# Who starts the first six query transfers of batch 1's cross attention: ScalarE or the sync engine

## The chip, the cores and the metric

The kernel runs on one core of a Trainium2 chip. The metric is the device time of one execution, in microseconds (us), and the time of a kernel is the median of several executions.

## The reference, cut to what matters

The whole computation is a chain of eight blocks on an input of two batches of 512 tokens with 128 features. Blocks 4 and 6 (counted from 0) are transformer stacks of six layers each, and the change lives in their layers, twelve in all. One layer is, for each batch:

```python
h = h + so_w @ attention(rope(q(n1(h))), rope(k(n1(h))), v(n1(h)))          # self: 16 heads of 8, 512 keys
h = h + co_w @ attention(rope(cq(n2(h))), rope(ck(context)), cv(context))   # cross: 154 keys
h = h + f2_w @ gelu(f1_w @ n3(h) + f1_b) + f2_b                             # feed-forward, 512 wide
```

n1, n2 and n3 are layer norms whose gain and shift depend on a condition vector. Block 0, a slot attention, is touched by the change in its semaphores alone.

## The kernel before, in words

Features lie on the 128 partitions and a batch's 512 tokens along the free axis. The kernel is written by hand as five instruction streams: TensorE (PE), VectorE (DVE), ScalarE (ACT), GpSimd (POOL) and the sync engine (SP), which only starts transfers. Semaphores join the streams. Each engine runs its own stream in order, so an instruction that waits holds up all that stands behind it on that engine.

A layer is 371 items of work (for instance a norm, a projection, a group of scores). The table PLACES (lines 85 to 137) gives each item a place in one common order, and each engine's stream is that order with the other engines' steps left out. Items of neighbouring layers may overlap: a place under 0 is done in the layer before, one from 371 on in the layer after.

**The stacking.** Attention scores are wanted almost in float32, but are computed in bf16. So a rotated query or key (L824, DVE) is split in three bf16 parts: the high part by an ACT copy (L715, item "hi"), the middle and the low part by three POOL operations (L881, L883, L886). The parts are then laid under each other on the partitions of the operand, six slots for each head, by transfers from on-chip memory to on-chip memory. For queries the high part goes to three slots, the middle one to two and the low one to one; each slot takes two transfers of 64 KB. That is twelve transfers for one batch's queries of one attention: six of part 0, four of part 1, two of part 2. They are started by `restack` (L424 to L434, the transfer itself is L433) from the items ("st", batch, unit, part), where unit 0 is the self queries, 1 the self keys, 2 the cross queries and 3 the cross keys.

Which engine starts them is set by the tuple ACT_STACKS (L436): the items in it are started by ACT (`stack`, L717 to L721), which waits for the high part first, the others by SP (L926 to L930), which waits for the part that the item needs. Before the change the tuple holds ("st", 0, 1, 0), batch 0's self keys, high part, and ("st", 1, 2, 0), batch 1's cross queries, high part.

**The order around the change.** The items are, by their places:

- 295 load sout (SP, eight transfers of weights)
- 296 proj(1,2), PE L574 and DVE L820 to L824: batch 1's cross queries
- 297 hi(1,2): ACT L715, then POOL
- 298 out(0,1): PE L536 and DVE L794, which finishes batch 0's h
- 299, 300, 301 the stack items of batch 1's cross queries, parts 0, 1 and 2
- 302 center(0,2): PE L552, ACT L694 and L695; the start of batch 0's third norm
- 303 var(0,2): PE L560, ACT L702 and L705; 304 apply(0,2): DVE L803 and L806, which makes xn
- 305 score(1,1,0,0): PE L460, the first scores of batch 1's cross attention; at this item PE waits for all twelve transfers (L442)
- 306, 308 f1(0,0) and f1(0,1): PE L616, ACT L757, with scores between them
- 316 f2(0): PE L631, DVE L849

ACT's stream holds the high part's copy, then the six transfers, then the squares of center(0,2). PE's stream holds center, var, the first scores, then f1.

A PE matmul of float32 operands shows as two instructions in the profile, so that f1(0,0), two matmuls, is "x4", and f2, four matmuls, "x8".

Of the kernel before, what the change touches and what calls it, by code (L numbers as in the profile page):

```python
# [253 lines left out]
def build(nc, dram):  # L254

    with ExitStack() as ctx:
# [176 lines left out]
                        eng.dma_start((kst if u == 1 else qst)[b][rows, :, :], unit_parts(b, u)[r::2, part, :])\  # L433
                           .then_inc(stacked(b, u), 16)  # L434

        ACT_STACKS = (("st", 0, 1, 0), ("st", 1, 2, 0))  # L436

        def stack_pe_items(pe, z):
            def score(it):
# [521 lines left out]
        def x_is(v):  # L961

            def wait(eng, b):
# [24 lines left out]
        sigma0 = carve(8)  # L988
        ITERS = 3
        s0 = {k: sem("slot_" + k) for k in  # L990
              ("loaded", "zeroed", "gained", "fold_mm", "folded", "kv_mm", "kv_out", "sigma", "slots", "q_mm", "q_scaled",
               "q_out", "logit_mm", "max", "max_scaled", "exp", "sum_inv", "attn", "col_mm", "upd_mm", "col_log", "col_inv",
               "upd_out", "lin_mm", "lin_out", "resid")}
        PER_ITER_RESID = 4
# [12 lines left out]
        def fold_pe(pe):  # L1007
            pe.wait_ge(s0["loaded"], 48)
            pe.transpose(bank(4)[:, 0:P], w0[:, WV], ident).then_inc(s0["fold_mm"], 1)
            pe.transpose(bank(5)[:, 0:P], bv_rows, ident).then_inc(s0["fold_mm"], 1)  # L1010
            pe.matmul(bank(6)[:, P:P + 1], w0[:, WQ], vec(V_QB), start=True, stop=True)
            pe.wait_ge(s0["gained"], 1)
            pe.matmul(bank(6)[:, 0:P], center, wq_gain, start=True, stop=True).then_inc(s0["fold_mm"], 1)
            pe.wait_ge(s0["folded"], 1)
            pe.matmul(bank(7)[:, 0:P], wv_turned, w0[:, WU], start=True, stop=True)
            pe.wait_ge(s0["folded"], 2)
            pe.matmul(bank(7)[:, P:2 * P], bv_turned, w0[:, WU], start=True, stop=True).then_inc(s0["fold_mm"], 1)
# [12 lines left out]
        def b0_pe(pe, c):  # L1030
            ln_pe(pe, c["ln"], x, x_is(c["x"]))
            fold_pe(pe)
            pe.wait_ge(loaded, LOADED)
            ln_pe(pe, c["ln"] + 1, ctxT[:, :], lambda eng, b: eng.wait_ge(ln_done, 2 * c["done"] + 2), width=CTX)
            pe.wait_ge(ln_done, 2 * c["done"] + 4)
            pe.wait_ge(s0["folded"], 6)
            pe.matmul(bank(4)[:, 0:B * CTX], w0[:, WK], ctxn, start=True, stop=True).then_inc(s0["kv_mm"], 1)
            for b in range(B):
                for k in range(KC):
                    n = key_rows(k)  # L1040
                    mm = pe.matmul(bank(5)[0:n, (2 * b + k) * P:(2 * b + k + 1) * P],
                                   ctxn[:, b * CTX + k * P:b * CTX + k * P + n], wvu, start=True, stop=True)
            mm.then_inc(s0["kv_mm"], 1)
            for t in range(ITERS):
                n = c["ln"] + 2 + 3 * t
                d = 2 * (c["done"] + 2 + t)
                for b in range(B):
                    slots_are(t)(pe, b)
                    pe.matmul(bank(b), center, cols(h, b), start=True, stop=True).then_inc(ln_centered, 1)
                for b in range(B):  # L1050
                    pe.wait_ge(ln_squared, 2 * n + b + 1)
                    pe.matmul(bank(2 + b), mean_w, cols(sq, b), start=True, stop=True).then_inc(ln_variance, 1)
                    pe.matmul(bank(6 + b), wq_fold, cols(h, b), start=True, stop=True).then_inc(s0["q_mm"], 1)
                pe.wait_ge(s0["kv_out"], 2)
                for b in range(B):
                    pe.wait_ge(s0["q_out"], 2 * t + b + 1)
                    for k in range(2 * b, 2 * b + 2):
                        n_rows = key_rows(k)
                        pe.matmul(bank(4 + k)[0:n_rows, :], key0[:, b * CTX + (k % 2) * P:b * CTX + (k % 2) * P + n_rows],
                                  cols(q0, b), start=True, stop=True).then_inc(s0["logit_mm"], 1)  # L1060
                pe.wait_ge(s0["zeroed"], 2)
                for b in range(B):
                    pe.wait_ge(s0["attn"], 4 * t + 2 * b + 2)
                    for k in range(KC):
                        mm = pe.matmul(bank(2 + b), mean_w, attn0[:, 2 * b + k], start=(k == 0), stop=(k == 1))
                    mm.then_inc(s0["col_mm"], 1)
                    for k in range(KC):
                        mm = pe.matmul(bank(b), val0[:, b, k], attn0[:, 2 * b + k], start=(k == 0), stop=(k == 1))
                    mm.then_inc(s0["upd_mm"], 1)
                ln_pe(pe, n + 1, h, lambda eng, b: eng.wait_ge(s0["resid"], PER_ITER_RESID * t + b + 1))  # L1070
                for b in range(B):
                    pe.wait_ge(ln_done, d + b + 1)
                    pe.matmul(bank(4 + b), w0[:, W1], cols(xn, b), start=True, stop=True).then_inc(s0["lin_mm"], 1)
                for b in range(B):
                    pe.wait_ge(s0["lin_out"], 2 * t + b + 1)
                    pe.matmul(bank(6 + b), w0[:, W2], cols(hid0, b), start=True, stop=True).then_inc(s0["lin_mm"], 1)
                ln_pe(pe, n + 2, h, lambda eng, b: eng.wait_ge(s0["resid"], PER_ITER_RESID * t + 2 + b + 1))

        def b0_act(act, c):
            ln_act(act, c["ln"])  # L1080
            act.wait_ge(s0["loaded"], 48)
            act.activation(sigma0[:, 0:1], vec(V_SIG), ACT.Exp).then_inc(s0["sigma"], 1)
            fold_act(act)
            ln_act(act, c["ln"] + 1, width=CTX)
            act.wait_ge(s0["kv_mm"], 1)
            act.activation(key0, bank(4)[:, 0:B * CTX], ACT.Identity, bias=vec(V_BK)).then_inc(s0["kv_out"], 1)
            for t in range(ITERS):
                n = c["ln"] + 2 + 3 * t
                ln_act(act, n)
                for k in range(4):  # L1090
                    r = key_rows(k)
                    act.wait_ge(s0["max_scaled"], 4 * t + k + 1)
                    act.wait_ge(s0["zeroed"], 2)
                    act.activation(attn0[0:r, k], bank(4 + k)[0:r, :], ACT.Exp, bias=smx0[0:r, k:k + 1],
                                   scale=float(D) ** 0.5, accum_out=sum0[0:r, k:k + 1]).then_inc(s0["exp"], 1)
                for b in range(B):
                    act.wait_ge(s0["col_mm"], 2 * t + b + 1)
                    act.activation(cols(lg, b), bank(2 + b), ACT.Ln).then_inc(s0["col_log"], 1)
                    act.wait_ge(s0["col_log"], 2 * t + b + 1)
                    act.activation(cols(rstd, b), cols(lg, b), ACT.Exp, scale=-1.0).then_inc(s0["col_inv"], 1)  # L1100
                ln_act(act, n + 1)
                for b in range(B):
                    act.wait_ge(s0["lin_mm"], 4 * t + b + 1)
                    act.activation(cols(hid0, b), bank(4 + b), ACT.Gelu, bias=vec(V_B1)).then_inc(s0["lin_out"], 1)
                both_log_and_exp(act)
                ln_act(act, n + 2)

        def b0_dve(ve, c):
            ve.memset(val0[:, :, :, :], 0.0).then_inc(s0["zeroed"], 1)
            ve.memset(attn0[:, :, :], 0.0).then_inc(s0["zeroed"], 1)  # L1110
            ve.wait_ge(s0["loaded"], 48)
            ve.tensor_scalar(wq_gain, w0[:, WQ], vec(V_QG), None, ALU.mult).then_inc(s0["gained"], 1)
            ln_dve(ve, c["ln"], xn)
            ve.wait_ge(s0["sigma"], 1)
            for b in range(B):
# [1 line left out]
                ve.tensor_scalar(cols(h, b), cols(xn, b), sigma0[:, 0:1], vec(V_MU), ALU.mult, ALU.add)\  # L1117
                  .then_inc(s0["slots"], 1)
            ve.wait_ge(loaded, LOADED)
            ve.tensor_scalar(b2_cond[:, 0:B], condT[:, :], vec(V_B2), None, ALU.add).then_inc(s0["gained"], 1)  # L1120
            ln_dve(ve, c["ln"] + 1, ctxn, gain=lambda b: vec(V_KG), shift=lambda b: vec(V_KB), width=CTX,
                   scaled=c["scaled"])
            ve.wait_ge(s0["kv_mm"], 2)
            ve.wait_ge(s0["zeroed"], 2)
            ve.wait_ge(s0["folded"], 6)
            ve.wait_ge(s0["gained"], 2)
            for k in range(4):
                r = key_rows(k)
                op = ve.tensor_tensor(val0[0:r, k // 2, k % 2], bank(5)[0:r, k * P:(k + 1) * P], bvu_rows[0:r, :], ALU.add)
# [18 lines left out]
            for t in range(ITERS):  # L1148
                n = c["ln"] + 2 + 3 * t
                sc = c["scaled"] + 1 + 2 * t  # L1150
                for b in range(B):
                    ve.wait_ge(ln_rstd, 2 * n + b + 1)
                    ve.wait_ge(s0["q_mm"], 2 * t + b + 1)
                    ve.tensor_tensor(cols(qraw0, b), bank(6 + b), cols(rstd, b), ALU.mult).then_inc(s0["q_scaled"], 1)
                    ve.wait_ge(s0["q_scaled"], 2 * t + b + 1)
                    ve.tensor_scalar(cols(q0, b), cols(qraw0, b), bq_fold[:, 0:1], None, ALU.add).then_inc(s0["q_out"], 1)
                largest(t, 0)
                largest(t, 1)
# [1498 lines left out]
```

## Time and profile before

| | |
|---|---|
| median of 3 runs | 3646.8 us (3642.5 to 3654.24) |
| the profiled execution's own time | 3644.69 us |
| its span, first to last instruction | 3642.9 us |
| mean granted TensorE clock | 0.916 of full speed |
| PE busy | 2960.6 us, 81% |
| DVE busy | 1979.4 us, 54% |
| ACT busy | 1896.2 us, 52% |
| POOL busy | 805.7 us, 22% |
| transfers L433 started by SP | 720 |
| transfers L433 started by ACT | 144 |

Busy time counts arithmetic alone: starting a transfer is not in it, though the engine can do nothing else meanwhile. In rows of the profile, "SPq" and "ACTq" are such starts. A row of the timeline merges like instructions in a row: start, length, engine, line, operation, output and inputs, count, and in brackets the idle time just before and what ended it. "issue" there means that the engine waited for nothing that the profile shows as a releaser.

### The profile page before, as it was taken

To read this page: it belongs to the slowest core of one execution; us is meant where nothing else is said; L and a number is where in the kernel's file an instruction comes from. 1 tells how busy PE (TensorE), PEld (TensorE's weight loads), DVE (VectorE), ACT (ScalarE), POOL (GpSimd) and SP (SyncE) were. 2 spreads that over 40 slices of the span, in tenths; PEclk is the share of its full clock that TensorE was granted. 3 is DMA by queue.
4 is the path that set the end of the run, shared out by engine and by line. 5 is a ranking of instruction groups with operands and counts; after the bars stand their busy time and mean duration, and the time that the engine had idled before them with its cause. 6 is when DMAs were issued, how large, how long until landed. Compare 5 with 4: busy or idle time off the path is not lost.

```text
span 3642.9 us, 50334 instructions
## 1 busy us (share of the span) xinstructions
PE 2960.6 (81%) x15559; PEld 1013.4 (28%) x15559; DVE 1979.4 (54%) x3535; ACT 1896.2 (52%) x2677; POOL 805.7 (22%) x1327
## 2 busy tenths in 40 slices
PE   7899999868788787887878746878788787887866
PEld 2463333222222222222222211222222222222225
DVE  4324444248375573756648366558375664846524
ACT  5432333327556474665747534647466574665632
POOL 0003444512212122122222102212212222222211
PEclk9999999979989898998989877989899998999977
DMA  1100000001110111101011001001110111101030
GB/s 41 53 18 6 1 1 1 10 20 39 33 35 24 36 36 32 36 27 48 20 36 41 22 8 43 25 29 41 33 35 27 38 30 31 42 23 48 24 115 7
DMA packets 125570, 110.74 MB, mean 30 GB/s; under 512 B 49982, under 2 KB 116076, under 8 KB 125292
## 3 DMA queue, kind: packets, MB, share of 16 engines
q1 hardware_dynamic: 114924, 97.80, 9.1%
q10 hardware_dynamic: 10368, 9.44, 0.8%
q8 instruction: 148, 2.42, 0.3%
q14 instruction: 130, 1.06, 0.1%
HBM read 41.96 MB, written 0.52 MB: 12 GB/s over the span
## 4 chain that ended last, share of the span: by engine, by line
PE 65%; DVE 15%; issue 7%; ACT 7%; POOL 3%; ACTq 2%; SPq 1%; DMA 0%; DVEq 0%; POOLq 0%
PE ps L508 11%; DVE arena L783 7%; PE ps L453 5%; PE ps L482 4%; PE ps L631 3%; PE ps L616 3%; PE ps L574 3%; PE ps L536 3%; PE ps L1452 3%; ACT arena L656 3%; PE ps L560 3%; PE ps L1468 3%; PE ps L525 2%; PE ps L552 2%; PE ps L516 2%
## 5 line engine op out<-in xcount | busy, mean ns | idle before, releaser
L656 ACT ACTIVATE arena<-ps 128x1024 f32<-128x1024 f32 x960 | 936.4, 1024 | 344.0 <-PE ps L482 340.3
L783 DVE TENSOR_REDUCE arena<-ps 128x1 f32<-128x512 f32 x1536 | 966.1, 683 | 207.1 <-PE ps L453 186.5
L508 PE MATMUL ps<-arena 128*32 128x512 f32 x3840 | 513.2, 609 | 20.5 <-ACT arena L656 18.0
L453 PE MATMUL ps<-arena 49*128 49x512 bf16 x1536 | 317.7, 410 | 239.5 <-DVE arena L783 198.4
L482 PE MATMUL ps<-arena 52*128 52x512 bf16 x1920 | 346.1, 387 | 28.7 <-ACT arena L656 25.2
L785 DVE TENSOR_REDUCE arena<-ps 128x3 f32<-128x462 f32 (+1 forms) x576 | 303.1, 579 | 108.7 <-PE ps L460 104.9
L865 POOL TENSOR_TENSOR arena<-arena,zeros 128x16 bf16<-128x16 f32 x192 | 42.3, 220 | 1078.7 <-DVE arena L783 636.7
L453 PEld LDWEIGHTS ps<-arena 49*128 49x128 bf16 x1536 | 75.2, 94 | 590.1 <-DVE arena L783 493.4
L875 POOL TENSOR_TENSOR arena<-arena 128x512 f32<-128x512 f32 x96 | 121.9, 1270 | 453.2 <-ACT arena L688 453.2
L881 POOL TENSOR_TENSOR arena<-arena 128x512 bf16<-128x512 f32 (+1 forms) x84 | 92.4, 1100 | 546.8 <-ACT arena L715 546.8
L803 DVE SCALAR_TENSOR_TENSOR tmp<-tmp,arena,rstd 128x512 f32<-128x512 f32 x72 | 54.1, 751 | 270.2 <-ACT rstd L705 267.9
L794 DVE TENSOR_TENSOR h<-ps,h 128x512 f32<-128x512 f32 x48 | 33.2, 692 | 299.1 <-PE ps L536 299.1
L1519 ACT ACTIVATE arena<-ps 128x1024 f32<-128x1024 f32 x96 | 98.0, 1021 | 177.7 <-PE ps L1456 141.7
L482 PEld LDWEIGHTS ps<-arena 52*128 52x128 bf16 x1920 | 86.8, 94 | 311.5 <-ACT arena L656 195.8
L536 PE MATMUL ps<-arena,w 128*128 128x512 f32 x192 | 128.8, 808 | 50.7 <-issue 23.8
L1680 POOL TENSOR_TENSOR arena<-arena 128x1024 f32<-128x1024 f32 x64 | 150.0, 2344 | 64.7 <-ACT arena L1519 64.2
L694 ACT ACTIVATE sq<-ps 128x512 f32<-128x512 f32 x76 | 45.2, 594 | 214.0 <-PE ps L552 160.6
L574 PE MATMUL ps<-xn,w 128*128 128x512 f32 x288 | 144.4, 627 | 8.0 <-DVE xn L806 7.4
L460 PE MATMUL ps<-arena 49*128 49x154 bf16 x1536 | 104.8, 237 | 56.1 <-DVE arena L785 38.3
L616 PE MATMUL ps<-xn,w 128*128 128x512 f32 x192 | 122.3, 772 | 20.7 <-DVE xn L806 20.7
L1587 DVE TENSOR_REDUCE arena<-ps 128x1 f32<-128x512 f32 x128 | 82.5, 686 | 101.9 <-PE ps L1420 101.9
L525 PE MATMUL ps<-arena,selector 128*128 128x512 f32 x192 | 106.8, 638 | 37.7 <-ACT arena L675 32.0
(379 smaller groups left out, 4185.7 us busy)
## 6 DMA issues: line engine op xcount, KB each, us to landing
arena<-arena SPq DMA_DIRECT2D x720, 64.0 KB
arena<-we_dram SPq DMA_DIRECT2D x24, 578.5 KB, 7.7
arena<-arena ACTq DMA_DIRECT2D x144, 64.0 KB
w<-weights_dram SPq DMA_DIRECT2D x26, 320.0 KB, 3.1
w<-weights_dram SPq DMA_DIRECT2D x13, 512.0 KB, 3.7
arena<-arena SPq DMA_DIRECT2D x384, 6.0 KB
arena<-arena SPq DMA_DIRECT2D x288, 19.2 KB
w<-weights_dram SPq DMA_DIRECT2D x39, 128.0 KB, 2.1
```

Of the source, the lines that this page charges most:

```text
L453: pe.matmul(s_bank(slot + r), qst[b][rows, idx, P * qt:P * (qt + 1)], kst[b][rows, idx, :], start=True, stop=True).then_inc(s_full, 1 + (z ...
L482: mm = pe.matmul(e_bank(slot)[:, S * r:S * (r + 1)], (kst, kstc)[a][b][rows, 2 * g + p, P * kt:P * (kt + 1)], qst[b][rows, 2 * g + p, :], ...
L508: mm = pe.matmul(bank(7)[32 * j:32 * j + 32, :], v, prob[:, slot, j, :], start=(g % 2 == 0 and kt == 0), stop=(a == 0 and g % 2 == 1 and k ...
L525: pe.matmul(e_bank(slot)[:, 0:S], selector2[:, :], osb[:, e, :], start=True, stop=True)\
L536: mm = pe.matmul(s_bank(slot), w[:, base + P * e:base + P * (e + 1)], att[:, b, e, :], start=(e == 0), stop=(e == 1))
L574: pe.matmul(s_bank(slot + i)[:, 0:B * CTX if u == 3 else S], w[:, base + P * i:base + P * (i + 1)], src, start=True, stop=True).then_inc(s ...
L616: mm = pe.matmul(e_bank(slot)[:, S * i:S * (i + 1)], w[:, W_F1 + P * t:W_F1 + P * (t + 1)], cols(xn, b), start=True, stop=True)
L656: act.activation(prob[:, chunk_no(b, a, g, kt) % NPROB, 2 * p:2 * p + 2, :], e_bank(slot).rearrange("p (j n) -> p j n", j=2), ACT.Exp, sca ...
L783: op = ve.tensor_reduce(nmax[:, g % 2, r, n:n + 1], s_bank(slot + r), AX.X, ALU.max, negate=True)
L785: op = ve.tensor_reduce(nmax[:, g % 2, r, 3 * n:3 * n + pack(n)], s_bank(slot + r)[:, 0:pack(n) * CTX].rearrange("p (i n) -> p i n", n=CTX ...
L875: gp.tensor_tensor(att[:, b, e, :], osb[:, e, :], rinv[:, e, :], ALU.mult).then_inc(att_ready, 1)
L1680: gp.tensor_tensor(sum2[0:n, :, :], sum2[0:n, :, :], prob2[0:n, j], ALU.add).then_inc(s2["summed"], 1)
```

## The change

The item ("st", 1, 2, 0) leaves ACT_STACKS: SP starts the six transfers of batch 1's cross queries' high part, at the same place 299 of its own order, and ACT no longer does. In block 0 semaphores are joined: "zeroed" and "gained" become "made", "q_scaled" and "q_out" become one, with the counts waited for adapted.

```diff
-        ACT_STACKS = (("st", 0, 1, 0), ("st", 1, 2, 0))
+        ACT_STACKS = (("st", 0, 1, 0),)
...
-              ("loaded", "zeroed", "gained", "fold_mm", "folded", "kv_mm", "kv_out", "sigma", "slots", "q_mm", "q_scaled",
+              ("loaded", "made", "fold_mm", "folded", "kv_mm", "kv_out", "sigma", "slots", "q_mm",
...
-            pe.wait_ge(s0["gained"], 1)
+            pe.wait_ge(s0["made"], 3)
...
-                    pe.wait_ge(s0["q_out"], 2 * t + b + 1)
+                    pe.wait_ge(s0["q_out"], 2 * (2 * t + b + 1))
...
-                pe.wait_ge(s0["zeroed"], 2)
+                pe.wait_ge(s0["made"], 2)
...
-            ve.memset(val0[:, :, :, :], 0.0).then_inc(s0["zeroed"], 1)
-            ve.memset(attn0[:, :, :], 0.0).then_inc(s0["zeroed"], 1)
+            ve.memset(val0[:, :, :, :], 0.0).then_inc(s0["made"], 1)
+            ve.memset(attn0[:, :, :], 0.0).then_inc(s0["made"], 1)
             ve.wait_ge(s0["loaded"], 48)
-            ve.tensor_scalar(wq_gain, w0[:, WQ], vec(V_QG), None, ALU.mult).then_inc(s0["gained"], 1)
+            ve.tensor_scalar(wq_gain, w0[:, WQ], vec(V_QG), None, ALU.mult).then_inc(s0["made"], 1)
...
-            ve.tensor_scalar(b2_cond[:, 0:B], condT[:, :], vec(V_B2), None, ALU.add).then_inc(s0["gained"], 1)
+            ve.tensor_scalar(b2_cond[:, 0:B], condT[:, :], vec(V_B2), None, ALU.add).then_inc(s0["made"], 1)
...
-            ve.wait_ge(s0["gained"], 2)
+            ve.wait_ge(s0["made"], 4)
...
-                    ve.tensor_tensor(cols(qraw0, b), bank(6 + b), cols(rstd, b), ALU.mult).then_inc(s0["q_scaled"], 1)
-                    ve.wait_ge(s0["q_scaled"], 2 * t + b + 1)
+                    ve.tensor_tensor(cols(qraw0, b), bank(6 + b), cols(rstd, b), ALU.mult).then_inc(s0["q_out"], 1)
+                    ve.wait_ge(s0["q_out"], 2 * (2 * t + b) + 1)
```

## Rows read from the trace of the kernel before

**Rows 1.** The page: the span, and the chain of waits by engine.

```profile
span 3642.9 us, 50334 instructions
...
PE 65%; DVE 15%; issue 7%; ACT 7%; POOL 3%; ACTq 2%; SPq 1%; DMA 0%; DVEq 0%; POOLq 0%
```

**Rows 2.** Waits, whole span: who waited for whom, us in total, times, longest.

```profile
ACT sq L694 <- issue: 52.8, 12, 4.4
...
PE ps L616 <- DVE xn L806: 17.9, 13, 2.8
PE ps L460 <- DMA arena<-arena: 12.3, 12, 1.5
```

**Rows 3.** Timeline of ACT in the second layer, around its transfers.

```profile
1164.46 0.63 ACT L715 ACTIVATE arena<-arena 128x512 bf16<-128x512 f32 x1 [2.05 <-DVE arena L824]
1165.12 4.28 ACTq L433 DMA_DIRECT2D arena<-arena  x6
1169.52 0.60 ACT L694 ACTIVATE sq<-ps 128x512 f32<-128x512 f32 x1 [4.42 <-issue]
```

**Rows 4.** Timeline of PE in the same layer.

```profile
1166.66 1.12 PE L552 MATMUL ps<-h,consts 128*128 128x512 f32 x2 [0.86 <-DVE h L794]
1170.24 1.12 PE L560 MATMUL ps<-sq,consts 128*128 128x512 f32 x2 [2.46 <-ACT sq L694]
1172.72 0.57 PE L460 MATMUL ps<-arena 49*128 49x154 bf16 x6 [1.36 <-DMA arena<-arena]
1174.19 3.78 PE L616 MATMUL ps<-xn,w 128*128 128x512 f32 x4 [0.89 <-DVE xn L806]
1177.90 0.56 PE L460 MATMUL ps<-arena 49*128 49x154 bf16 x6
1178.39 1.98 PE L616 MATMUL ps<-xn,w 128*128 128x512 f32 x4
```

**Rows 5.** Timelines of SP and POOL in the same layer.

```profile
1166.35 4.15 SPq L433 DMA_DIRECT2D arena<-arena  x6
...
1167.57 1.15 POOL L886 TENSOR_TENSOR arena<-arena 128x512 bf16<-128x512 f32 x1
```

**Rows 6.** Line L433, whole span: ns of one start, least/median/most; first and last.

```profile
L433 SPq DMA_DIRECT2D arena<-arena x720: 607/608/1462, 779.3 to 3456.3; - x180
L433 ACTq DMA_DIRECT2D arena<-arena x144: 622/708/1219, 782.9 to 3455.2; - x144
```

**Rows 7.** Timeline of SP, where it starts ten and twelve transfers on its own.

```profile
1050.16 6.53 SPq L433 DMA_DIRECT2D arena<-arena  x10
...
1071.96 7.88 SPq L430 DMA_DIRECT2D arena<-arena  x12
```

**Rows 8.** Timelines of SP and PE at the first stack's start.

```profile
779.31 12.11 SPq L433 DMA_DIRECT2D arena<-arena  x18
...
793.18 0.61 PE L453 MATMUL ps<-arena 49*128 49x512 bf16 x2 [13.31 <-DMA arena<-arena]
```

**Rows 9.** ACT and PE timelines in the first layer and the last (twelfth).

```profile
947.58 4.31 ACTq L433 DMA_DIRECT2D arena<-arena  x6
...
955.19 0.57 PE L460 MATMUL ps<-arena 49*128 49x154 bf16 x6 [1.02 <-DMA arena<-arena]
...
3451.65 4.27 ACTq L433 DMA_DIRECT2D arena<-arena  x6
...
3459.29 0.56 PE L460 MATMUL ps<-arena 49*128 49x154 bf16 x6 [1.54 <-DMA arena<-arena]
```

**Rows 10.** DMA by stretch: us, five engines' busy, PEclk, DMA share, GB/s.

```profile
1166.40:1170.50 4.10, 1.38 (x3) 0.56 (x4) 0.13 (x1) 0.98 (x2) 2.18 (x2) 1.00 0.45 137
1051.20:1056.70 5.50, 5.04 (x31) 1.30 (x23) 5.07 (x9) 3.15 (x4) 3.26 (x7) 1.00 0.33 96
```

**Rows 11.** f2 by stretch, second and third layer; columns as in rows 10.

```profile
1184.01:1187.70 3.69, 3.69 (x9) 1.50 (x9) 0.64 (x2) 0.00 (x0) 0.83 (x4) 1.00 0.35 92
...
1403.01:1408.40 5.39, 5.39 (x9) 2.09 (x9) 0.64 (x2) 0.00 (x0) 0.83 (x4) 0.68 0.24 63
```

More of the change, by code:

```diff
@@ L1092, in b0_act @@
                     act.wait_ge(s0["max_scaled"], 4 * t + k + 1)
-                    act.wait_ge(s0["zeroed"], 2)
+                    act.wait_ge(s0["made"], 2)
                     act.activation(attn0[0:r, k], bank(4 + k)[0:r, :], ACT.Exp, bias=smx0[0:r, k:k + 1],
@@ L1123, in b0_dve @@
             ve.wait_ge(s0["kv_mm"], 2)
-            ve.wait_ge(s0["zeroed"], 2)
+            ve.wait_ge(s0["made"], 2)
             ve.wait_ge(s0["folded"], 6)
-            ve.wait_ge(s0["gained"], 2)
+            ve.wait_ge(s0["made"], 4)
             for k in range(4):
```

## The prediction, made before the changed kernel was seen

> **What bounds the kernel now.** I began with the page's chain of waits [rows 1]. PE carries 65% of the chain, but 2% of it is ACTq, ACT starting transfers: such starts lie on the path that sets the end. The list of waits says where [rows 2]. ACT's squares at L694 stood behind "issue" 12 times, 52.8 us in total, 4.4 us each, once in each layer of the two stacks. In the same places PE waits for transfers before its first cross scores (L460, 12 times, 12.3 us) and for xn before f1 (L616, 17.9 us in 13 waits; the longest, 2.8 us, lies between the stacks, the twelve of the layers sum to 15.1 us).
>
> The timelines of the second layer show how these hang together. I count from the start of ACT's six transfers, 1165.12, as zero.
>
> - ACT: the high part's copy is done at 0, its six starts last to 4.28, and the squares begin at 4.40 [rows 3]. PE had delivered their input at 2.66 (1166.66 + 1.12 = 1167.78) [rows 4]. So center(0,2) loses 4.40 - 2.70 = 1.70 us to the starts.
> - SP: it starts its own six, parts 1 and 2, at 1.23, when POOL has the middle part, and is done at 5.38 [rows 5]. The last one opens PE's wait at 7.60, 2.22 us later, and the first scores run [rows 4, 5].
> - f1 starts at 9.07, held by xn, which stems from the squares; PE idles 0.89 us in front of it [rows 4].
>
> So two legs run side by side and meet at f1: ACT's leg (starts, squares, var, xn) ends at 9.07, the transfers' leg (SP's starts, landing, scores) would allow f1 at 7.60 + 0.49 = 8.09. The 0.49 is what f1(0,1) stands behind the scores ahead of it at the same low clock (1178.39 - 1177.90) [rows 4]. The leg of ACT is the later one now, by about 1 us.
>
> **Part 1, what is taken from ACT.** Six starts of 0.708 us [rows 6], 4.28 us a layer. The squares begin 1.70 us earlier, at 2.70, as L552's end sets it, and xn is ready near 9.07 - 1.70 = 7.37. The rest of the freed time covers nothing: ACT's next work needs f1. Worth at most 1.7 us a layer, and only if nothing else holds f1.
>
> **Part 2, what is given to SP.** SP waits for the high part at place 299 (its loads for sout are long done) and can begin at 0.03. It has then all twelve to start. A start lasts 0.608 us on SP at the median [rows 6], but they don't stand back to back: ten of this very kind took 6.53 us, twelve others 7.88 us, 0.66 us each [rows 7]. The middle part is ready at 1.2 and the low part at 3.60 (1167.57 + 1.15 - 1165.12) [rows 5], well before SP gets to them after six and ten starts, so no data wait remains. SP is done at 0.03 + 7.88 = 7.91, against 5.38 before: 2.53 us later. Nothing else of SP's stands in the way or is needed soon; its next step is a row for scores that are not yet computed.
>
> **Part 3, from the last start to PE.** The trace has two values. In the layers, with ACT and SP both starting, it is 2.22 us. At the start of the first stack, where SP alone starts the last seven or so of 18, PE goes at 793.18, 1.76 us after SP's end at 791.42 [rows 8]. The DMA engines bear this out: their share is 0.45 and 137 GB/s while two engines start, 0.33 and 96 GB/s with SP alone [rows 10], so less stands in line. After the change SP starts alone, so I take 1.76 and keep 2.22 as the bound. The first scores then start at 7.91 + 1.76 = 9.67, against 7.60 before: +2.07. Over the layers the 7.6 holds: 955.19 - 947.58 = 7.61 in the first, 3459.29 - 3451.65 = 7.64 in the last [rows 9], 7.43 to 7.68 in the ten between.
>
> **Part 4, what reaches f1.** xn, at 7.4, no longer matters; f1 follows the scores. In the second layer it starts at 9.67 + 0.49 = 10.16 against 9.07: +1.09. Over all twelve layers: the scores are 12 x 2.08 = 25.0 us later, and of that the waits for xn absorb what they sum to, 15.1 us [rows 2], and 12 x 0.07 us more (modelled ends overlap: the scores show as 0.57 but f1 can follow at 0.49 to 0.52). That leaves 25.0 - 15.1 - 0.8 = +9.1 us, 0.76 us a layer.
>
> **Part 5, what follows.** PE is in order, and behind f1 come the scores of batch 1's cross attention, f2, the next layer's norm; all of it waits for f1 directly or behind it in PE's stream. I see no later wait for something that doesn't shift, so nothing gives it back.
>
> **Part 6, the clock.** f1's first two matmuls run at 1.2 GHz already (3.78 us, against 1.98 for the second two [rows 4]), since PE was mostly idle ahead of them. After the change the idle stretches are joined: var moves to about 3.5, then PE idles from 4.6 to 9.7, and then works without a gap. So f1 is mostly at the low level before and after. f2 is the sensitive one: at 2.4 GHz it takes 3.69 us, in other layers 5.39 us with a granted clock of 0.68 [rows 11]. Five of the twelve layers are of the first kind, seven of the second. Which it is depends on when PE's work falls, so a shift of 0.8 us can flip layers both ways. I take zero; the bounds are 5 x 1.7 = +8.5 us and 7 x 1.7 = -11.9 us.
>
> **Part 7, the semaphores of block 0.** The counts open the same waits at the same instructions: wq_gain is DVE's third "made", and the two memsets precede it on DVE anyway. Nothing is added, 0 us.
>
> **The page's rule.** SP alone keeps the DMA engines a third busy [rows 10], so here the starts are the scarce thing, at 0.66 us each against six by ACT beside them. The Trainium skill, page "DMA: Bandwidth & Descriptors", section "Issuing engines are not separate DMA queues", says that all starts end on the same 16 engines, and that starting from several saves only the time of starting, "which is usually small relative to the DMA itself". The trace agrees with the first half and not with "small". By the rule at its word the landing wouldn't move, which is rival A.
>
> **The sum.** Own time 3644.7 + 9.1 = 3653.8. The median of the runs shown is 2.1 us above that execution, so 3646.8 + 9.1 = 3655.9. About 0.3%, 10.9 us (3635.9 to 3657.7), is what a measurement of this kernel can tell from no change; the forecast lies just inside, on the slow side.
>
> **Lower and upper bounds of the terms.** Starts back to back would be 12 x 0.608 = 7.30 instead of 7.88: -7.0 us in twelve layers, sum +2.1. A landing of 2.22 instead of 1.76: +5.5 us, sum +14.6.
>
> **Rivals.**
>
> A. Transfer-bound, faster. If the 16 engines and not the starts set the last landing, the scores start as before, f1 moves up to right behind them and the twelve waits for xn vanish: -15.1 - 0.8 = -15.9, 3630.9. For it: two starting engines lengthen the landing from 1.76 to 2.22. Against it: a share of 0.45 is no full queue, and SP cannot hand over its twelfth transfer before 7.3. Chance 0.05.
>
> B. The clock, slower. Its place is f2(0), L631. If the later and unbroken idle ahead of the scores makes the clock rise later relative to f1, all twelve f2 fall in the 5.39 us kind: +8.5 on top: 3646.8 + 9.1 + 8.5 = 3664.4. It decides from the point where more than one of the five fast layers flips and none flips back. For it: seven of twelve are already so. Against: nothing in the rows makes the flip one-sided. Chance 0.25.
>
> C. The clock the other way, or denser starts: seven slow f2 become fast, 3646.8 + 9.1 - 11.9 = 3644.0; or starts back to back, 3648.9. Chance 0.15.
>
> D. The forecast, 3650 to 3661: chance 0.55, of which about 0.33 lie under 3657.7.
>
> That the change does nothing can't be: the item moves in all twelve layers.
>
> **The numbers.** Faster: A, 0.05. Within 0.3%: C and the lower part of D, 0.15 + 0.33, and a little of B, 0.50 in all. Slower: the rest of D and B, 0.45. The range leaves out A and the ends of B and C: 3643 to 3666. Predicted 3655.9.
>
> **What would show it.** In the changed trace: no "issue" in front of L694, squares about 2.7 us after the copy's end; one SP row of twelve starts, 7.9 us, from the copy's end; PE's first cross scores at 9.7 after it with a wait for DMA of about 5 us; f1 right behind without a wait for xn; L631 still of both kinds. It is wrong if the scores start under 8.5 (A), if SP's twelve take 7.3, or if the period of a layer grows by anything but 0.8 us, which f2's lengths would then explain.

## The result, and the profile after

The changed kernel takes 3656.9 us (median of 12 runs, 3646.5 to 3664.1), the kernel before 3646.4 beside it (12 runs). The ratio is 1.0028, with a 95% interval from 1.0017 to 1.0038: slower by 10 us (6 to 14). Measured again beside the kernel before, the changed kernel gave 1.0012 (1.0002 to 1.0022), slower by 4 us (1 to 8). The forecast was 3655.9, on the slow side of no change.

The profiled execution took 3662.74 us, near the slow end of its runs, so I compare layer with layer and not span with span. The page, as far as it answers to [rows 1]:

```profile
span 3660.9 us, 50334 instructions
...
PE 2963.8 (81%) x15559; PEld 1015.1 (28%) x15559; DVE 1981.7 (54%) x3535; ACT 1899.6 (52%) x2677; POOL 806.0 (22%) x1327
...
PE 65%; DVE 15%; issue 7%; ACT 6%; SPq 3%; POOL 3%; DMA 1%; ACTq 0%; DVEq 0%; POOLq 0%
```

ACTq has left the chain (2% before) and SPq has grown from 1% to 3%, DMA from 0 to 1%: the starts are on the path still, under another engine's name. The waits over the whole span, and line L433 (ns of one start), against [rows 2, 6]:

```profile
ACT sq L694 <- PE ps L552: 197.8, 38, 18.5
...
PE ps L460 <- DMA arena<-arena: 61.1, 13, 5.4
...
PE ps L616 <- DVE xn L806: 5.6, 2, 2.8
...
L433 SPq DMA_DIRECT2D arena<-arena x792: 607/608/1781, 782.0 to 3475.1; - x198
L433 ACTq DMA_DIRECT2D arena<-arena x72: 622/699/1219, 784.5 to 3295.0; - x72
```

The 52.8 us of "issue" ahead of L694 are gone, its waits are for PE alone. PE's wait for transfers at L460 has grown from 12.3 to 61.1 us, to 5 us a layer. The twelve waits for xn ahead of f1 have vanished. (The row for them in [rows 2] is of the stretch of the two stacks alone, 780 to 3510 us; over the whole span the kernel before has 20.7 us in 14 waits, and the two that are left here lie outside these places.) So the later leg at f1 has changed hands. The second layer shows it in its timelines, ACT first, then PE, SP and a stretch of the DMA engines (columns as in rows 10), against [rows 3, 4, 5, 10]:

```profile
1169.55 0.63 ACT L715 ACTIVATE arena<-arena 128x512 bf16<-128x512 f32 x1 [2.06 <-DVE arena L824]
1172.90 0.60 ACT L694 ACTIVATE sq<-ps 128x512 f32<-128x512 f32 x1 [2.73 <-PE ps L552]
...
1171.75 1.12 PE L552 MATMUL ps<-h,consts 128*128 128x512 f32 x2 [0.86 <-DVE h L794]
...
1179.83 0.57 PE L460 MATMUL ps<-arena 49*128 49x154 bf16 x6 [5.08 <-DMA arena<-arena]
1180.32 3.37 PE L616 MATMUL ps<-xn,w 128*128 128x512 f32 x4
...
1183.93 1.98 PE L616 MATMUL ps<-xn,w 128*128 128x512 f32 x4
...
1189.55 5.39 PE L631 MATMUL ps<-arena,w 128*128 128x512 f32 x8 [0.31 <-DVE arena L785]
...
1170.20 7.88 SPq L433 DMA_DIRECT2D arena<-arena  x12
...
1171.50:1177.50 6.00, 2.24 (x4) 0.59 (x4) 1.35 (x3) 3.69 (x5) 2.17 (x2) 0.90 0.35 100
```

Zero here and below is 0.03 us behind the copy's end, where the first start stands or stood (1170.21 in this layer, 1165.12 in the kernel before): SP's twelve starts run to 7.87, PE sees the last transfer at 9.62, f1 starts at 10.11 with nothing between. The squares start at 2.69. The DMA engines are a third busy, at 100 GB/s.

### The profile page after: what moved, and what is told of

Read it like the earlier page. It is cut to its first block, busy times and chain, and to the rows that moved or that the text cites. A ratio compares the mean times of both kernels' runs of the same rounds, so it can differ in the third digit from the quotient of the medians.

```text
span 3660.9 us, 50334 instructions
## 1 busy us (share of the span) xinstructions
PE 2963.8 (81%) x15559; PEld 1015.1 (28%) x15559; DVE 1981.7 (54%) x3535; ACT 1899.6 (52%) x2677; POOL 806.0 (22%) x1327
## 4 chain that ended last, share of the span: by engine, by line
PE 65%; DVE 15%; issue 7%; ACT 6%; SPq 3%; POOL 3%; DMA 1%; ACTq 0%; DVEq 0%; POOLq 0%
PE ps L508 10%; DVE arena L783 7%; PE ps L453 5%; PE ps L482 4%; PE ps L616 3%; PE ps L631 3%; SPq L433 3%; PE ps L574 3%; PE ps L536 3%; PE ps L1452 3%; ACT arena L656 3%; PE ps L1468 3%; PE ps L525 2%; PE ps L560 2%; PE ps L552 2%
## 5 line engine op out<-in xcount | busy, mean ns | idle before, releaser
L460 PE MATMUL ps<-arena 49*128 49x154 bf16 x1536 | 105.0, 238 | 104.6 <-DMA arena<-arena 61.1
L574 PE MATMUL ps<-xn,w 128*128 128x512 f32 x288 | 143.4, 622 | 8.0 <-DVE xn L806 7.4
L694 ACT ACTIVATE sq<-ps 128x512 f32<-128x512 f32 x76 | 45.3, 596 | 198.3 <-PE ps L552 197.8
L820 DVE TENSOR_TENSOR arena<-ps,rope 128x512 f32<-128x512 f32 x144 | 99.5, 692 | 66.0 <-PE ps L574 63.0
```

What stands on the lines that cost most here:

```text
L574: pe.matmul(s_bank(slot + i)[:, 0:B * CTX if u == 3 else S], w[:, base + P * i:base + P * (i + 1)], src, start=True, stop=True).then_inc(s ...
```

## The experiments

All times in this table are means over the twelve layers, in us from the zero just named, read from the timelines of one profiled execution each. The ratio is to the kernel before, run on the same chip, with its 95% interval. "12 x f1" is what the shift of f1 against the 9.41 of before would give, if all behind it shifted as much. An execution that was profiled can lie some us off its kernel's median: 5.9 us above it for the changed kernel, 5.4 and 8.5 above with three and five starts by ACT.

| kernel | starts by ACT / SP | squares | scores | f1 | f2 ends | slow f2 | 12 x f1 | ratio |
|---|---|---|---|---|---|---|---|---|
| before | 6 / 6 | 4.37 | 7.59 | 9.41 | 23.81 | 7 | | 1 |
| changed | 0 / 12 | 2.72 | 9.65 | 10.15 | 24.51 | 4 | +8.9 | 1.0028 (1.0017 to 1.0038) |
| changed, again | 0 / 12 | 2.72 | 9.64 | 10.14 | 24.71 | 5 | +8.8 | 1.0012 (1.0002 to 1.0022) |
| sems_only | 6 / 6 | 4.37 | 7.63 | 9.31 | 23.70 | 6 | -1.2 | 0.9993 (0.9984 to 1.0002) |
| split2 | 2 / 10 | 2.72 | 8.48 | 8.96 | 23.36 | 6 | -5.4 | 0.9995 (0.9985 to 1.0004) |
| split3 | 3 / 9 | 2.72 | 7.91 | 8.39 | 22.45 | 2 | -12.2 | 0.9986 (0.9974 to 0.9998) |
| split4 | 4 / 8 | 2.80 | 7.47 | 7.93 | 21.95 | 2 | -17.8 | 0.9967 (0.9955 to 0.9979) |
| split4, again | 4 / 8 | 2.80 | 7.47 | 7.95 | 21.95 | 1 | -17.5 | 0.9959 (0.9945 to 0.9973) |
| split5 | 5 / 7 | 3.61 | 7.28 | 8.44 | 22.27 | 1 | -11.6 | 0.9990 (0.9978 to 1.0002) |
| drop3 | 0 / 9 | 2.72 | 7.67 | 8.14 | 21.97 | 0 | -15.2 | 0.9965 (0.9953 to 0.9978) |
| drop6 | 0 / 6 | 2.72 | 7.02 | 7.64 | 21.95 | 4 | -21.2 | 0.9933 (0.9918 to 0.9948) |
| order_after | 0 / 12 | 2.72 | 10.89 | 7.36 | 24.74 | 12 | -24.6 | 1.0092 (1.0076 to 1.0107) |
| order_before | 6 / 6 | 4.37 | 13.13 | 9.45 | 25.78 | 12 | +0.5 | 1.0105 (1.0090 to 1.0121) |

"Slow f2" counts the layers in which L631 took 5.0 us or more instead of 3.7: 5.39 or 5.40 in most kernels, 5.05 to 6.60 in the two exchanged ones. In drop3 and drop6 transfers are left out, so part of the operand is not written and the output is not the reference's.

**The semaphores alone.** The changed kernel with ACT_STACKS as before.

```diff
-        ACT_STACKS = (("st", 0, 1, 0),)
+        ACT_STACKS = (("st", 0, 1, 0), ("st", 1, 2, 0))
```

> The semaphores of block 0 are joined as in the change, but ACT keeps the six starts. Theory (two legs meet at f1; the change is slower only because SP starts twelve transfers at 0.66 us each): the time of the kernel before, ratio 1.000, within 0.999 to 1.001; f1 at 9.4 us after the high part's copy. Rival (the joined counts, or anything in block 0, carry part of the loss): ratio up to 1.003 with f1 still at 9.4.

Ratio 0.9993, and f1 at 9.31. Block 0's part of the change costs nothing that can be measured; the loss belongs to the moved starts.

**The six starts shared.** The first of the six go to ACT, the rest to SP at the same place, with a wait for the high part on each engine; the number is 2, 3, 4 or 5.

```diff
-        def restack(eng, b, u, part):
-            for slot in slots_of(u, part):
-                for r in range(2):
+        SHARED, BY_ACT = ("st", 1, 2, 0), 4
+
+        def restack(eng, b, u, part, which=slice(0, None)):
+            for slot, r in [(slot, r) for slot in slots_of(u, part) for r in range(2)][which]:
+                if True:
...
+                elif it == SHARED:
+                    act.wait_ge(part_hi, z.after("hi", ("hi", b, u), it))
+                    restack(act, b, u, part, slice(0, BY_ACT))
...
-                    restack(sp, b, u, part)
+                    restack(sp, b, u, part, slice(BY_ACT if it == SHARED else 0, None))
```

> As the changed kernel, but ACT starts two of the six transfers of the high part and SP the other ten. Theory: SP's ten end at 0.03 + 10 x 0.66 = 6.6, the first scores start 1.75 later at about 8.35, f1 at 8.85 after the copy's end; xn is ready by 7.7. That is 0.55 us less than the 9.41 of before and 1.3 less than the 10.15 of the change: -6.6 us against before, ratio 0.998. Rival (transfers are bound by the 16 DMA engines, not by the starts): scores stay at about 9.6 as in the changed kernel, no gain. Rival (the loss of the change is the clock at f2): f1 moves but the time does not follow.

> ACT starts three of the six, SP nine. Theory: SP ends at 5.95 to 6.1, scores at 7.9, f1 at 8.4, xn at 7.7 (squares not held): 1.0 us under before and between two and four starts by ACT: -11 us, ratio 0.997. Rival (transfer-bound): no difference from two or four.

> ACT starts four of the six, SP eight. Theory: SP's eight end at 5.3, scores 1.8 to 2.2 later at 7.1 to 7.5, f1 possible at 7.6 to 8.0; ACT's four starts end at 2.85, the squares begin at 3.0 (0.25 us late), xn allows f1 at 9.41 - 1.4 = 8.0. f1 at 8.0, 1.4 us under before: -17 us, ratio 0.9953. This is where the legs should meet. Rival (transfer-bound): scores and f1 where the change has them, 1.003. Rival (only ACT's release counts, SP's queue is free): equal to the gain without SP's leg, 12 x 1.65 = -20 us.

> ACT starts five of the six, SP seven. Theory: ACT's leg is the later one again: five starts end at 3.6, the squares begin at 3.7, xn allows f1 at 8.7; SP ends at 5.3, the scores at 7.5. f1 at 8.7, 0.7 us under before, 0.8 over four starts by ACT: -8 us, ratio 0.998. Rival (the more ACT starts the better): faster than with four.

f1 came out at 8.96, 8.39, 7.93 and 8.44, against 8.85, 8.4, 8.0 and 8.7 expected. The minimum lies at four, where the theory has the legs meet: with two or three SP's leg is the later one, with five ACT's (squares at 3.61 instead of 2.72). "Transfer-bound" falls, since the same bytes land 2.2 us earlier when two engines start them; "the more ACT starts the better" falls with five. Four starts by ACT, in the second layer (ACT, PE, SP; the added lines make L460 of before L462, L616 L618 and L433 L435):

```profile
1165.82 2.61 ACTq L435 DMA_DIRECT2D arena<-arena  x4
1168.54 0.60 ACT L696 ACTIVATE sq<-ps 128x512 f32<-128x512 f32 x1 [2.75 <-PE ps L554]
...
1173.40 0.57 PE L462 MATMUL ps<-arena 49*128 49x154 bf16 x6 [3.02 <-DMA arena<-arena]
1173.90 3.78 PE L618 MATMUL ps<-xn,w 128*128 128x512 f32 x4
...
1165.81 5.65 SPq L435 DMA_DIRECT2D arena<-arena  x8
```

ACT's four starts end at 2.61, before PE has the squares' input ready: here they are free (over the twelve layers the squares start at 2.80, against 2.72 with none). SP's eight end at 5.64. Both are what shortens f1's wait.

The time is another matter. Four starts gave 0.9967 and 0.9959, 12 and 15 us under before on the two chips, where f1's shift says 17.8. Two, three and five starts gave -2, -5 and -4 us where it says -5, -12 and -12. So the ratios expected for two, three and four (0.998, 0.997, 0.9953) all lie below the measured intervals, and with two starts the time cannot be told from that of before: there the rival by which f1 moves and the time does not is not refuted. More on that below.

**Starts left out.** Three or all six of the high part's transfers are started by nobody; the wait counts are lowered to match.

```diff
+SHORT, LEFT_OUT = ("st", 1, 2, 0), 3
...
+        n -= 16 * LEFT_OUT if item == SHORT else 0
...
-            for slot in slots_of(u, part):
-                for r in range(2):
+            for slot, r in [(slot, r) for slot in slots_of(u, part) for r in range(2)][LEFT_OUT if ("st", b, u, part) == SHORT else 0:]:
+                if True:
```

> As the changed kernel, but three of SP's six starts of the high part are left out (three of the 48 slot rows per half keep what stood there; the output is of that). SP starts nine, ACT none. Theory: SP ends at 5.95 after the copy, the scores start at 7.7, f1 at 8.2 with xn ready at 7.4 to 7.7: 2.0 us a layer under the change, 1.2 under before: -14 us, ratio 0.996, less what the clock takes. Rival (it is the order of engines, or ACT's help, that counts and not the number of SP's starts): f1 near 10.

> All six transfers of the high part are left out and nobody starts them; SP starts the six of the middle and low part from 1.23 on, as before the change. Theory: both legs are short, SP ends at 5.3, scores at 7.1, the squares at 2.7 and xn at 7.4 to 7.7, so f1 at 7.6 to 7.7, -1.75 us a layer: -21 us, ratio 0.9942. This is the most that this place can give. Rival (the clock sets the time of this stretch): f1 moves, f2's lengths grow by as much and the ratio stays above 0.998.

Nine starts by SP alone put the scores at 7.67 and f1 at 8.14: twelve starts less three is 1.98 us, 0.66 each. So the number of SP's starts sets f1, and ACT's help is not needed for it. Nor is it the three transfers fewer: with three starts by ACT and nine by SP all twelve are made, and the scores start at 7.91, only 0.24 us later. With six left out both legs are short (PE, then SP, in the second layer; zero is 1167.21):

```profile
1174.23 0.57 PE L462 MATMUL ps<-arena 49*128 49x154 bf16 x6 [2.47 <-DMA arena<-arena]
1174.73 3.78 PE L618 MATMUL ps<-xn,w 128*128 128x512 f32 x4
...
1168.49 3.96 SPq L435 DMA_DIRECT2D arena<-arena  x6
```

f1 starts at 7.52 here and the time falls by 0.67%, 24 us, as the 21 from f1's shift say within the interval (19 to 30). This is about what the place holds; four starts by ACT get half of it or more.

**f1 ahead of the scores.** Two places exchanged, in the changed kernel and in the one before.

```diff
-    ('score', 1, 1): [[305, 307, 309], [310, 311, 314], [319, 323, 324], [328, 330, 334]],
+    ('score', 1, 1): [[306, 307, 309], [310, 311, 314], [319, 323, 324], [328, 330, 334]],
...
-    ('f1',): [[306, 308], [382, 384]],
+    ('f1',): [[305, 308], [382, 384]],
```

> The changed kernel with two places exchanged: f1(0,0) at 305 and the first scores of batch 1's cross attention at 306, so PE does not stand in front of f1 for the twelve transfers. Theory: the transfers land as in the change (scores possible at 9.6), but f1 starts when xn is ready, 7.7 after the copy's end, and the scores follow it at about 11.5: f1 1.7 us earlier than before, the scores lose nothing that was not lost behind f1: second half of f1 at about 12.0 against 13.4 before. -1.4 us a layer, -17 us, ratio 0.995. Rival (what counts is when the scores reach DVE, whose reductions are behind them): scores at 11.5 instead of 7.6 give +3.9 less what f1 took, slower than before, ratio 1.005 or more.

> The kernel before with the same exchange of places: f1(0,0) ahead of batch 1's first cross scores. The transfers land at 7.6 as before, but the scores now stand behind f1, which xn holds to 9.4. Theory (behind f1 the scores' reductions on DVE are the next leg, which set f2's start in the exchanged kernel): scores at 11.4 to 13.1, f2 starts 8.5 later at about 20 to 21.5 instead of 19.1, slower than before by 1 to 2.4 us a layer or more, ratio 1.004 to 1.01. Rival (the exchanged kernel was slow only for the late transfers, or for the clock alone): ratio 1.000, f2's start near 19.

My theory had the first one 17 us faster; it was 0.92% slower than before, about 34 us, and the rival named there is what came. The second had its theory borne out: the scores start at 13.13, f2 at 20.47 (20 to 21.5 expected, 19.12 before), and the kernel is 1.05% slower, 38 us. So it takes no late transfers to make the exchange cost time. PE in the first layer of the exchanged changed kernel, then of the exchanged kernel before:

```profile
960.53 1.98 PE L616 MATMUL ps<-xn,w 128*128 128x512 f32 x4 [2.81 <-DVE xn L806]
962.73 0.37 PE L460 MATMUL ps<-arena 49*128 49x154 bf16 x6 [0.22 <-DMA arena<-arena]
963.90 0.38 PE L460 MATMUL ps<-arena 49*128 49x154 bf16 x6 [0.80 <-DVE arena L785]
964.21 1.98 PE L616 MATMUL ps<-xn,w 128*128 128x512 f32 x4
...
969.82 6.60 PE L631 MATMUL ps<-arena,w 128*128 128x512 f32 x8
...
962.28 3.78 PE L616 MATMUL ps<-xn,w 128*128 128x512 f32 x4 [2.81 <-DVE xn L806]
966.00 0.56 PE L460 MATMUL ps<-arena 49*128 49x154 bf16 x6
...
973.28 5.40 PE L631 MATMUL ps<-arena,w 128*128 128x512 f32 x8 [0.24 <-DVE arena L785]
```

f1 does start at 7.36 in the mean, near the 7.7 expected. But two score groups now stand in a row ahead of f1(0,1), and in this layer the second waits 0.80 us for DVE to empty its banks; the reductions that used to run beside f1 run with PE idle. f2 then starts at 19.40 against 19.12, in spite of an f1 that was 2.05 us earlier, and it is of the slow kind in all twelve layers of both kernels. In eight layers of the exchanged changed kernel f1(0,1) is slow as well, 3.46 to 3.78 us instead of 1.98. Why f2 is always slow there, and where the rest arises (f2's end is 0.9 and 2.0 us later a layer, 11 us of 34 and 24 of 38), is not settled. By the mean granted clock of all their executions the two kernels spend 94 and 79 us more at the low clock than the kernel before on the same chip, so the clock has its part.

**The two confirmations.**

> The changed kernel once more on the chip of the others. Theory: 1.002 to 1.004 of before, f1 at 10.1 after the copy in each layer. Rival (the loss was the clock of one chip): 1.000.

> The kernel with four starts by ACT and eight by SP once more, beside the changed kernel and the one before on one chip. Theory: again 0.9955 to 0.998 of the time before, 11 to 13 us under it, and some 20 us under the changed kernel. Rival (the first result owed to where the clock fell on that chip): within 0.2% of before.

The changed kernel came out at 1.0012, under the 1.002 to 1.004 expected, with the same f1 to 0.01 us. The rival's 1.000 lies just outside its interval (1.0002 to 1.0022). The version with four starts came out at 3632.8 us against 3647.6 for before and 3653.5 for the change: it beats both.

**The clock gives back.** Why does the time follow f1 only in part in the shared kernels? Stretches of 40 us from the copy's end, two layers of the kernel before, then two of split4, again; the column after POOL's is the granted clock:

```profile
1165.00:1205.00 40.00, 30.52 (x158) 10.45 (x158) 19.07 (x35) 20.33 (x30) 7.19 (x20) 0.91 0.10 30
1205.00:1245.00 40.00, 26.25 (x93) 7.91 (x89) 17.26 (x26) 13.95 (x20) 9.94 (x12) 0.74 0.14 42
1384.00:1424.00 40.00, 30.51 (x154) 10.51 (x153) 17.84 (x33) 18.72 (x28) 6.73 (x19) 0.87 0.10 30
1424.00:1464.00 40.00, 26.47 (x97) 8.54 (x95) 18.50 (x28) 15.62 (x23) 10.40 (x12) 0.83 0.14 42
...
1166.00:1206.00 40.00, 31.57 (x166) 11.09 (x164) 19.95 (x36) 20.79 (x30) 7.86 (x21) 0.91 0.10 30
1206.00:1246.00 40.00, 25.22 (x91) 7.75 (x87) 18.58 (x28) 13.42 (x20) 9.15 (x11) 0.76 0.14 42
1384.00:1424.00 40.00, 31.68 (x163) 11.11 (x163) 19.59 (x35) 20.62 (x31) 7.63 (x20) 0.91 0.10 30
1424.00:1464.00 40.00, 25.25 (x95) 7.86 (x89) 18.61 (x29) 13.82 (x20) 9.55 (x12) 0.77 0.15 42
```

In the kernel before, a layer with a fast f2 (the one from 1165) has 0.91 and then 0.74; one with a slow f2 (from 1384) has 0.87 and then 0.83. With four starts by ACT five of the six layers read this way are of the first kind. So part of what a fast f2 wins is lost at the low clock 40 us later. In that second stretch, in the layer from 1165, PE's waits are for DVE (5.3 us in five waits), ACT (3.0 us in two) and POOL (2.9 us in one).

One profiled execution is a thin witness for the clock. But each execution's own mean granted clock is on record, and twice what it lacks of 1, times the span, is its time at the low level (1.2 GHz). The third column is the mean of that over all executions, less the same for the kernel before on the same chip. Among the executions of the kernel before on one chip, a us more at the low level goes with 0.23 to 0.28 us more time (a fit over 15 to 23 executions, on three chips). The fourth column is an estimate from that: the shift of f1, and a quarter of the third column.

| kernel | 12 x f1, us | more at the low level, us (standard error) | both | measured, us (interval) |
|---|---|---|---|---|
| changed, again | +8.8 | -9 (5) | +7 | +4 (1 to 8) |
| sems_only | -1.2 | -4 (3) | -2 | -3 (-6 to 1) |
| split2 | -5.4 | +9 (4) | -3 | -2 (-5 to 1) |
| split3 | -12.2 | +15 (4) | -8 | -5 (-9 to -1) |
| split4 | -17.8 | +2 (7) | -17 | -12 (-16 to -8) |
| split4, again | -17.5 | -1 (3) | -18 | -15 (-20 to -10) |
| split5 | -11.6 | +31 (5) | -4 | -4 (-8 to 1) |
| drop3 | -15.2 | +2 (5) | -15 | -13 (-17 to -8) |
| drop6 | -21.2 | -34 (3) | -30 | -24 (-30 to -19) |

With two, three and five starts the clock is thus enough for the difference, within the noise. With four it is not: their time at the low level is that of before, and 3 to 5 us are still missing, just beyond the interval in one of the two measurements. That gap is open. drop6 lies at the edge of its interval and fits the shift of f1 alone better. And that the low clock costs this much is read from executions that differ by chance, not from an experiment on the clock.

## Why the prediction was right

- **Part 1** (squares 1.70 us earlier) was right: they start at 2.69 in the second layer, 2.72 in the mean, and xn is ready at 7.24 (predicted 7.37, which was f1's start 0.13 us behind xn). Nothing came of it, as predicted.
- **Part 2** (twelve starts in 7.88 us) was right to 0.01 us in ten layers; in the last layer of each stack they took 8.2.
- **Part 3** (landing at 1.76 and not 2.22) was right: 1.75 in the second layer, 1.73 in the mean. The choice of the value from the one place where SP started alone decided 5.5 us of the sum. The DMA share fell from 0.45 to 0.35, as the row of SP alone had it. drop3 and the shared kernels bear out the rest.
- **Part 4** (f1 0.76 us later) was right: 10.15 against 9.41 is 0.74, or +8.9 us for the twelve layers where the sum had 9.1.
- **Part 5** (all behind f1 shifts with it) came out at f2's end, 0.70 and 0.90 us later, but in part by luck, for two things nearly cancel there. f2 starts 1.13 us later (20.25 against 19.12), 0.39 more than f1, and is shorter by 0.42 us in the mean. It would not have held for a gain of the same size: split3 shows 1.4 us a layer at f2's end and 5 us in all. The sign set for this, a layer's period growing by 0.8 us, was not met either: over the ten layers with another behind them it went from 218.5 to 219.7 us, and to 219.5 when measured again, and f2, shorter in the mean, does not explain it.
- **Part 6** (the clock at zero) was a fair centre with the wrong picture behind it. Slow f2 went from seven to four or five layers, and by the bounds I set that should have won some 4 us. It won nothing, since in six of the eight layers with a fast f2 the low clock fell on f1(0,1) just ahead of it: 2.66 to 2.81 us instead of 1.98, at a granted clock of 0.70 to 0.74. Before, one layer of twelve was like that. The layer from 2808.96 of the changed kernel, whose f1(0,1) and f2 are to be held against the 1.98 and 5.39 above:

```profile
2823.27 2.81 PE L616 MATMUL ps<-xn,w 128*128 128x512 f32 x4
...
2829.71 3.69 PE L631 MATMUL ps<-arena,w 128*128 128x512 f32 x8 [0.31 <-DVE arena L785]
```

  My bounds of -11.9 and +8.5 counted f2 alone.
- **Part 7** (semaphores) was right: 0.9993.
- **Rival A** (transfer-bound), by which the landing would not move, fell by 2.1 us at the scores, and the shared kernels show why: who starts, and how many, sets the landing. The Trainium skill, page "DMA: Bandwidth & Descriptors", section "Issuing engines are not separate DMA queues", calls what starting from several engines saves usually small beside the DMA itself. The trace does not agree with that here: the twelve starts take 7.87 of the 9.62 us that pass until PE has the last transfer. **Rival B** (all f2 slow) did not come with this change, but it did come in both exchanged kernels.

Two measurements of the same pair, about +10 us (6 to 14) and +4 us (1 to 8), lie on both sides of the +8.9 from f1. What is shown is a loss of some 4 to 10 us with this cause. That the first came within 1 us of the forecast is luck; the second is half of it, and what moves between them was put down to the clock above by an estimate, not by a test.

## What to carry to other kernels

Where the start of a transfer costs an engine 0.6 to 0.7 us, twelve of them are a term of the critical path. Set out both legs, the engine's own next work and the last landing, and share the starts so that the legs meet; starts that end before the engine's next input is ready are free. Moving all of them to the idle engine only moved the wait. And check what else stands behind an in-order wait before moving it: with f1 ahead of the scores the changed kernel started f1 2.8 us sooner and became 0.92% slower than before instead of 0.1 to 0.3%.

## What the hardware showed that I had not expected

- Starts slow each other when two engines make them: eight by SP beside four by ACT took 5.65 us (0.71 each), twelve by SP alone 7.88 (0.66 each). The six of parts 1 and 2 took 4.15 us beside ACT's six and 3.96 alone (drop6).
- The time from SP's last start to PE's scores grows with how long ACT goes on starting: 1.73 us in the mean with none by ACT, 1.75, 1.76, 1.85 and 1.97 with two to five, 2.19 with six.
- The granted clock traded one stretch for another: 0.91 and 0.74, or 0.87 and 0.83, in neighbouring 40 us. A stretch that gets its full clock back is no gain by itself.
- The idle time just ahead of an instruction does not tell its clock. In the exchanged changed kernel f1 starts at 7.36 after 2.8 us of idle in all twelve layers; in the first it ran at 2.4 GHz (1.98 us for four, granted clock 1.00), in the other eleven it took 3.45 to 3.78 us, mostly at 1.2 GHz.
